# Mixture of experts in a four-layer kernel: routed groups of 384 rows through DRAM in place of every expert for every token

## The reference

```
scores = sigmoid(xt @ gate_w.T)                     # 4096 tokens, 16 experts
_, idx = top_k(scores + gate_b, 4)
w = take_along_axis(scores, idx);  w = 2.5 * w / sum(w)
comb[token, idx] = w                                # 0 for the 12 others
for e in 16 experts:
    h = silu(xt @ w1_e.T) * (xt @ w3_e.T)           # 128 hidden
    y = y + comb[:, e] * (h @ w2_e.T)
y = y + shared expert(xt)
```

## Time and profile before

| what | us |
|---|---|
| median of 3 runs | 1736.63 (1736.21 to 1738.77) |
| the profiled execution | 1737.69 |
| its span, first to last instruction | 1735.9 |
| TensorE busy | 1439.8 (83%) |
| VectorE busy | 1275.1 (73%) |
| ScalarE busy | 636.4 (37%) |
| GpSimd busy | 326.5 (19%) |
| mean granted TensorE clock, share of full speed | 0.93 |

### The profile page before, as it was taken

The page is one execution under the profiler, slowest core; times in us unless marked ns, Lnnn a source line. Parts: engine busy times, 40 slices in busy tenths (PEclk is TensorE's granted clock), DMA queues, the critical chain, the costliest instruction groups (busy, mean ns, idle before and its releaser), DMA issues. The chain is left out here.

```text
span 1735.9 us, 33621 instructions
## 1 busy us (share of the span) xinstructions
PE 1439.8 (83%) x10080; PEld 756.7 (44%) x10080; DVE 1275.1 (73%) x2834; ACT 636.4 (37%) x936; POOL 326.5 (19%) x340
## 2 busy tenths in 40 slices
PE   4799955999999999999997947887878788888766
PEld 2455532555555555555554522332333233232455
DVE  4999855878787777877667637887878788785475
ACT  0455531111111111111113412665656666666530
POOL 2433332112111121111002050111111111111110
PEclk7999976999999999999998965999999999899998
DMA  5011000000000000000004761111211111110002
GB/s 182 19 37 36 19 1 0 0 0 0 0 0 0 0 0 0 0 0 0 1 0 131 213 170 34 34 34 47 55 35 34 50 51 34 33 34 2 1 0 97
DMA packets 54738, 60.00 MB, mean 35 GB/s; under 512 B 6398, under 2 KB 41982, under 8 KB 54666
## 3 DMA queue, kind: packets, MB, share of 16 engines
q1 hardware_dynamic: 49466, 54.62, 11.1%
q10 hardware_dynamic: 5200, 4.33, 0.8%
HBM read 36.34 MB, written 22.28 MB: 34 GB/s over the span
## 5 line engine op out<-in xcount | busy, mean ns | idle before, releaser
L1461 DVE TENSOR_REDUCE small<-ps 128x1 f32<-128x480 f32 (+6 forms) x768 | 419.2, 596 | 99.7 <-PE ps L1513 91.4
L1439 ACT ACTIVATE region<-ps 128x1024 f32<-128x1024 f32 (+5 forms) x384 | 322.9, 880 | 229.9 <-PE ps L1570 228.2
L956 PE MATMUL ps<-region 128*128 (+1 forms) x1632 | 378.5, 382 | 8.0 <-issue 7.5
L788 ACT ACTIVATE region<-ps 128x512 f32<-128x512 f32 x136 | 81.2, 597 | 446.8 <-PE ps L960 408.8
L956 PEld LDWEIGHTS ps<-region 128*128 (+1 forms) x1632 | 158.9, 98 | 178.4 <-issue 15.9
L1586 PE MATMUL ps<-region 128*32 128x512 f32 (+5 forms) x1792 | 196.7, 512 | 28.3 <-POOL region L1411 21.6
L970 PE MATMUL ps<-region 128*128 (+1 forms) x1632 | 201.7, 273 | 19.6 <-DVE region L896 18.1
L1513 PE MATMUL ps<-region 48*128 48x480 f16 (+6 forms) x896 | 158.7, 344 | 45.6 <-DVE small L1461 44.8
L970 PEld LDWEIGHTS ps<-region 128*128 128x128 f16 x1632 | 156.7, 98 | 63.1 <-DVE region L896 19.4
L1411 POOL TENSOR_SCALAR_AFFINE_SELECT region<-region 128x512 f32<-128x512 f32 (+2 forms) x160 | 87.7, 549 | 491.5 <-ACT region L1439 491.5
L1570 PE MATMUL ps<-region 50*128 50x512 f16 (+5 forms) x896 | 133.7, 334 | 12.7 <-issue 10.5
(11 more groups left out here) (196 smaller groups left out, 1708.6 us busy)
## 6 DMA issues: line engine op xcount, KB each, us to landing
v_parts<-region SPq DMA_DIRECT2D x16, 576.0 KB, 5.8
region<-v_parts SPq DMA_DIRECT2D x16, 576.0 KB, 3.9
region<-k_parts SPq DMA_DIRECT2D x96, 68.0 KB, 2.2
region<-q_parts SPq DMA_DIRECT2D x96, 64.0 KB, 2.1
k_parts<-region SPq DMA_DIRECT2D x16, 272.0 KB, 3.3
x_sb<-in_x ACTq DMA_DIRECT2D x8, 512.0 KB, 9.4
region<-in_w13T SPq DMA_DIRECT2D x16, 256.0 KB, 2.9
q_parts<-region SPq DMA_DIRECT2D x16, 256.0 KB, 3.3
```

Source lines behind the costliest of these rows:

```text
L956: ins = nc.tensor.matmul(o, w(wt, kh, half_), xt[:, kh, cols], start=n == 0, stop=n == 5)
L1439: nc.scalar.activation(dst, src, ACT.Exp, scale=SCALE).then_inc(s_exp, 1)
L1461: nc.vector.tensor_reduce(nmp[:, qt, half, p0:p0 + np_, place], bank[:, 0:np_ * nk].rearrange("p (h k) -> p h k", h=np_), AX.X, ALU.max).t ...
```

## The change

The router now also keeps, for each token, its four experts and their weights. Each token's normalised row (high and low part, 256 words), its four experts and its number are one row of 261 words. The 16 experts have a region each in a DRAM tensor `xs`; a running count says at which place of its expert's region a token's row belongs, and GpSimd scatters the row to its four places with indirect DMAs, 128 rows each, 16 for a chunk. The shared expert alone is computed for all tokens, in the same loop over the 8 chunks. When all rows are in DRAM, tables are made from the counts: for each of 58 groups of 384 rows its expert and its first row (58 is the most that 16 x 1024 rows of 16 experts can need; a group beyond the last points at a spare region that holds no token). SyncE fills the end of each region with empty rows and loads the groups into 4 buffers. For a group TensorE does 12 transposes, 12 gate and up matmuls of 384 columns and 9 down matmuls with the weights of the expert, whose number it reads into a register. VectorE finds where each row's result belongs (`homes`), and GpSimd scatters the 384 results to `ys` with 3 indirect DMAs; rows of no token are dropped by the bounds check. The relayout then fetches the four results of each token (2 MB for a chunk) and adds them to x, each by its weight, before it normalises (`combine`).

The diff, cut; ScalarE's part, the router's arithmetic and the tables are left out:

```diff
+GROUP = 3 * P
+GROUPS = (B * L * TOPK + E * (GROUP - 1)) // GROUP
+ROW = D + TOPK + 1
+ROW_BUFS = 4
+G_BUFS = 4
+Y_BUFS = 3
...
             @block.sync
+                for b in range(ROW_BUFS):
+                    sp.wait_ge(s_sent[b], CHUNKS // ROW_BUFS * TC * TOPK * 16)
+                sp.wait_ge(s_tabs, 3)
+                def fill_tail(e):
+                    first = sp.value_load(tail_tab[0:1, e:e + 1], ...)
+                    sp.dma_start(xs[bass.ds(first, GROUP), :]..., flat(fill)).then_inc(s_tail[e], 16)
+                for e in range(FILLS_AHEAD):
+                    fill_tail(e)
+                for g in range(GROUPS):
+                    if g + FILLS_AHEAD < E:
+                        fill_tail(g + FILLS_AHEAD)
+                    if g < E:
+                        sp.wait_ge(s_tail[g], 16)
+                    if g >= G_BUFS:
+                        sp.wait_ge(s_gTps, g - G_BUFS + 1)
+                        sp.wait_ge(s_home, g - G_BUFS + 1)
+                    first = sp.value_load(start_tab[0:1, g:g + 1], ...)
+                    sp.dma_start(flat(xg[:, g % G_BUFS]), xs[bass.ds(first, GROUP), :]...)
...
             @block.gpsimd
+                for c in range(CHUNKS):
+                    if c + 2 < CHUNKS:
+                        rstd_of(c + 2)
+                    pool.wait_ge(s_slot, c + 1)
+                    for j in range(TC):
+                        for r in range(TOPK):
+                            nc.gpsimd.indirect_dma_start(out=xs, ..., in_=rows[:, b, j, :], ...).then_inc(s_sent[b], 16)
+                for g in range(GROUPS):
+                    b = g % Y_BUFS
+                    pool.wait_ge(s_home, g + 1)
+                    pool.wait_ge(s_yout, g + 1)
+                    for j in range(GT):
+                        nc.gpsimd.indirect_dma_start(
+                            out=ys, out_offset=bass.IndirectOffsetOnAxis(ap=home[:, b, j:j + 1], axis=0),
+                            in_=y_out[:, b, j, :], in_offset=None, bounds_check=B * L * TOPK - 1,
+                            oob_is_err=False).then_inc(s_back[b], 16)
...
             @block.vector
+                for c in range(CHUNKS):
+                    choose(c)
+                    if c + 2 < CHUNKS:
+                        statistics(c + 2)
+                    hidden(c)
+                    slots(c)
+                    hidden_low(c)
+                    if c + 2 < CHUNKS:
+                        normalised(c + 2)
+                    add_shared(c)
...
+                def homes(g):
+                    b, v = g % G_BUFS, g % 2
+                    dve.wait_ge(s_xg[b], (g // G_BUFS + 1) * 16)
+                    order.mark(nc.vector.scalar_tensor_tensor(out=which[:, v], ...))
+                    order.wait()
+                    order.mark(nc.vector.tensor_reduce(rank_of[:, v, :], which[:, v], AX.X, ALU.add))
+                    order.wait()
+                    if g >= Y_BUFS:
+                        dve.wait_ge(s_back[g % Y_BUFS], g // Y_BUFS * GT * 16)
+                    nc.vector.tensor_tensor(home[:, g % Y_BUFS, :], rank_of[:, v, :], ...).then_inc(s_home, 1)
+                def group_hidden(g):
+                    dve.wait_ge(s_gsilu, g + 1)
+                    nc.vector.scalar_tensor_tensor(out=hg_buf[:, g % 2, :], in0=ps[...], ...).then_inc(s_gh, 1)
+                    dve.wait_ge(s_ghh, g + 1)
+                    nc.vector.tensor_tensor(hgl[:, g % 2, :], hg_buf[:, g % 2, :], hgh[:, g % 2, :],
+                                            ALU.subtract).then_inc(s_ghl, 1)
+                def group_out(g):
+                    dve.wait_ge(s_gy, g + 1)
+                    nc.vector.tensor_copy(y_out[:, g % Y_BUFS]..., ps[:, 6:8, :]...).then_inc(s_yout, 1)
+                homes(0)
+                homes(1)
+                group_hidden(0)
+                for g in range(GROUPS):
+                    if g + 2 < GROUPS:
+                        homes(g + 2)
+                    if g + 1 < GROUPS:
+                        group_hidden(g + 1)
+                    group_out(g)
...
             @block.tensor
+                for g in range(GROUPS):
+                    now = ahead
+                    if g + 2 < GROUPS:
+                        group_transposes(g + 2)
+                    if g + 1 < GROUPS:
+                        ahead = expert(g + 1)
+                        group_gate_up(g + 1, ahead)
+                    group_down(g, now)
...
+                def fetch(c):
+                    pool.wait_ge(s_comb, c * TC * TOPK + 1)
+                    nc.gpsimd.dma_start(yg[:]..., ys[0:B * L * TOPK, :]...).then_inc(s_yg, 16)
...
+                def combine(c):
+                    dve.wait_ge(s_yg, (c + 1) * 16)
+                    for r in range(TOPK):
+                        for j in range(TC):
+                            if r:
+                                hold(dve, s_comb, c * TC * TOPK + 1 + n - TC + 1, s_tick)
+                            nc.vector.scalar_tensor_tensor(out=tile_of(c * TC + j), in0=yg[:, j, r, :], scalar=w,
+                                                           in1=tile_of(c * TC + j), op0=ALU.mult, op1=ALU.add).then_inc(s_comb, 1)
                 def normalise(order, b, h):
+                    combine(b * 2 + h)
```

More of the change, by code:

```diff
@@ L747, in flamingo, with flat @@
             CHUNKS = 2 * B
[L748 to L764, removed]
+            def flat(t):
+                return t.rearrange("p a n -> p (a n)")
@@ L766, in _, with rstd_of @@
             @block.gpsimd
             def _(pool):
[L768 to L772, removed]
+                def rstd_of(c):
+                    pool.wait_ge(s_var, c + 1)
+                    nc.gpsimd.tensor_tensor(rstd[:], ve[:], half[:], ALU.pow).then_inc(s_rstd, 1)
@@ L774, in _ @@
+                for b in range(Y_BUFS):
+                    pool.wait_ge(s_back[b], len(range(b, GROUPS, Y_BUFS)) * GT * 16)
             @block.scalar
             def _(act):
[L776 to L806, removed]
@@ L941, in comb_transposed @@
[L941 to L952 removed]
+                three = ((0, 0), (1, 0), (0, 1))
@@ new lines, in transposes @@
+                def transposes(c):
+                    if c:
+                        pe.wait_ge(s_xT, 2 * c)
+                    for part in range(2):
+                        pe.wait_ge((s_hi, s_lo)[part], c + 1)
+                        for k in range(KH):
+                            for j in range(TC):
+                                ins = nc.tensor.transpose(xT_ps[part][:, k, j * P:(j + 1) * P],
+                                                          halves(rows, c % ROW_BUFS)[:, j, part, k * P:(k + 1) * P], identh[:])
+                        ins.then_inc(s_xTps, 1)
@@ new lines, in _ @@
+                transposes(0)
+                logits(0)
+                for c in range(CHUNKS):
+                    shared_gate_up(c)
+                    ranks(c)
+                    if c + 1 < CHUNKS:
+                        transposes(c + 1)
+                        logits(c + 1)
+                    shared_down(c)
+                pe.wait_ge(s_slot, CHUNKS)
+                nc.tensor.matmul(count_ps, counts[:, CHUNKS, :], onesb[:, 0:1], start=True, stop=True)
+                nc.tensor.matmul(row_ps, onesb[:, 0:1], counts[:, CHUNKS, :], start=True, stop=True).then_inc(s_count, 1)
@@ new lines, in group_gate_up @@
+                def group_gate_up(g, e):
+                    pe.wait_ge(s_gT, 2 * g + 2)
+                    if g >= 2:
+                        pe.wait_ge(s_gh, g - 1)
+                    for half_ in range(2):
+                        n = 0
+                        for kh in range(KH):
+                            for part, low in three:
+                                w = flat((w13h, w13l)[low][:, bass.ds(e, 1), kh * D + half_ * P:kh * D + half_ * P + P])
+                                ins = nc.tensor.matmul(ps[:, 2 + 2 * (g % 2) + half_, 0:GROUP], w, xgT[:, g % 2, part, kh, :],
+                                                       start=n == 0, stop=n == 5)
+                                n += 1
+                    ins.then_inc(s_ggu, 1)
@@ new lines, in group_down @@
+                def group_down(g, e):
+                    pe.wait_ge(s_ghl, g + 1)
+                    if g:
+                        pe.wait_ge(s_yout, g)
+                    for j in range(GT):
+                        for n, (part, low) in enumerate(three):
+                            ins = nc.tensor.matmul(ps[:, 6 + j // 2, (j % 2) * D:(j % 2 + 1) * D],
+                                                   (hgh, hgl)[part][:, g % 2, j * P:(j + 1) * P],
+                                                   flat((w2h, w2l)[low][:, bass.ds(e, 1), :]), start=n == 0, stop=n == 2)
+                    ins.then_inc(s_gy, 1)
```

579 lines of the change are left out of this document (376 added, 203 removed).

## The result

The changed kernel takes 1881.8 us (median of 4 runs, 1879.7 to 1883.2) against 1736.4 before: 1.083 times as long, 95% interval 1.082 to 1.085. The forecast was 1911 us, with a range of 1745 to 2120 and a chance of 0.83 for slower.

The account below looks back on a forecast made before the run. TensorE was taken to bound the experts' stage before the change, GpSimd's scatters and a chain of waits after it. 243.1 + 191 + 12 + 540 + 824.6 + 100 = 1910.7 us of span, so 1911 us; range 1745 to 2120.

Parts of the forecast that it names:

- A: Router and shared expert, 8 chunks: GpSimd's 16 scatters per chunk set the pace, 20.5 us a chunk, 191 us in all.
- behind A: Between router part and groups: SyncE waits for every scatter, stores tails and loads the first group, 12 us.
- C: The 58 groups: scatters, landing, homes, hidden layer and eviction form a chain without overlap, 9.1 us a group, 540 us.
- D: Relayout: single-buffered fetches of 2.1 MB and four additions per token add 100 us, bounds 80 and 140.
- The unseen price: The time one scatter of 128 rows holds GpSimd: taken as 1.2 us, ends 0.42 and 2.0.
- The clock: In the groups: TensorE at its lower clock level needs 7.8 us a group, under the 9.1 us period, so doesn't decide.
- The DMA engines: In the groups about 0.8 MB move in 9.1 us; engines busy over 80% there or in A would show the forecast wrong.
- The rule on GpSimd's descriptors: VectorE's fast operations block GpSimd's DMA descriptors: in the router part at most 1.4 us a chunk, 11 us in all.
- Cheap scatters: Rival, same chain in the groups: a scatter takes 0.42 us, period 6.3, total 1719 us, faster; chance 0.14.
- 3t + L: In the groups: three scatters' GpSimd time plus the last one's landing; under 3.5 us, cheap scatters would decide.
- Dear ones: Rival: a scatter takes 2.0 us and its landing 3, period 12.1 us, sum 2187 + 2; chance 0.14.
- the third rival: In the groups: no chain holds, TensorE paces them at 5.1 us with a register load, total 1680 us; chance 0.03.

## Why the prediction was right

The sign, the mechanism and, within 1.6%, the time were right; that the time came so near is partly luck, since several terms were off in opposite directions. By the forecast's own steps, in us of span:

| part | forecast | measured |
|---|---|---|
| A, to SyncE's first tail (443.1) | 191 | 200 |
| behind A, to the first rows of a group (453.6) | 12 | 10.5 |
| C, to the relayout (960.1) | 540 | 506.5 |
| D, the relayout's addition | 100 | 98.8 |
| the rest, against before | 0 | -3.6 |

*The unseen price* was 1.2 us for a scatter. It is 0.96 + 0.30 = 1.26 in A and 1.28 in C: the chosen row (0.55 for GpSimd's smallest work) and the engines' 0.50 for 128 rows gave the size, but for a wrong reason, since 64 rows cost 0.92. In A it makes 8 x 16 x 0.06 = 8 of the 9 us that were missing; the first scatter started at 268.6, 25.5 us into the stage in place of 24, and makes the rest. Scatters that were held up (5.2 us in all, below) and roots that don't fall into this part (five are there, of eight forecast) cancel out.

*Part C*, step by step: scatters 3.55 (forecast 3.6); landing 1.55 in place of 2.4; from `homes` to the end of `group_out` 2.65 in place of 3.0; then 0.88 us from the eviction's end to the scatter's start (0.87 to 0.91 in 54 of the 58 groups), where I had a hop of 0.1. Sum 8.63 against 9.1. Two terms were mis-sized in opposite directions: the landing taken from SyncE's stores of 256 KB was 0.9 too long, and GpSimd's start 0.8 too short. Over all groups: 55 periods of 8.61 in place of 9.1 are 27 us less. No wait follows the last three, which take 11.3 us in place of 27.3: 16 less. Filling the pipeline took 14.4 (453.6 to 468.0) in place of 12, and 7.0 us at the block's end, 953.1 to 960.1, were not in the forecast. Together 33.5 less.

*The clock.* At the lower level TensorE was to need 7.8 us for a group, under the period, and so decide nothing. In the groups it was granted 0.83 and was busy for 58%; moving the wait, which added no speed to TensorE, took the period to 3.88 and the clock to 1.00. The step held. One sign did not: TensorE was to be busy for less than half, and was for 58%. A group took it 279.2 / 58 = 4.8 us at that clock, in place of 3.9; at a granted 1.00, with the moved wait, it was 3.7. It stayed off the path all the same.

*The DMA engines.* They were to stay under 80%. They had a share of 0.28 in A and 0.26 in the groups, but 0.83 (276 GB/s) in the 26 us between, with the first loads and tails. The forecast set 0.8 MB in 9.1 us, 87 GB/s, at less than half of the relayout's 171; it is just over half, and 82 were measured.

*Part D.* 33 us before the first q matmul and 67 behind it were forecast (61, and 6 for the clock). The first q matmuls after the change:

```profile
1007.97 2.31 PE L1463 MATMUL ps<-region 128*128 128x512 f16 x5 [3.41 <-DVE region L1412]
```

That is 47.9 us behind the block's start (960.1), where 47 were forecast, in place of 14.6: 33 more. From there to the attention's first load it is 155.4 us in place of 89.8 (925.9 to 1015.8), 66 more. Both parts held. Inside the second the shape was otherwise: the first stores of q in two successive batches lie 44.5, 43.5 and 30.0 us apart, where 46, 40 and 40 were forecast, and the first store stands 21.5 us behind the first matmul, before the change 9.7, since the fetch and the additions of the next chunk come ahead of the splits on VectorE.

*The rule on GpSimd's descriptors.* In four of the eight chunks of A a scatter is held up behind the subtraction that makes the low part (L959). Timeline of the kernel after: first a scatter beside the subtraction that is not held up, then, a chunk later, two that are, the first beside a normalisation (L954):

```profile
292.83 1.30 DVE L959 TENSOR_TENSOR region<-xn,region 128x1024 f16<-128x1024 f32 x1 [1.12 <-ACT region L875]
292.87 0.96 POOL L853 DMA_INDIRECT expert_rows<-region,small  x1 [0.30 <-issue]
...
311.36 1.41 DVE L954 TENSOR_SCALAR xn<-x_sb,mv,rstd 128x256 f32<-128x256 f32 x4 [7.17 <-POOL rstd L835]
311.52 1.16 POOL L853 DMA_INDIRECT expert_rows<-region,small  x1 [0.20 <-issue]
...
313.95 1.23 DVE L959 TENSOR_TENSOR region<-xn,region 128x1024 f16<-128x1024 f32 x1 [1.18 <-ACT region L875]
314.25 1.77 POOL L853 DMA_INDIRECT expert_rows<-region,small  x1 [0.30 <-issue]
```

A scatter that starts 0.3 us into the subtraction takes 1.77 us in place of 0.96, and one beside the normalisation 1.16: 1.0 us for each of these four chunks. Two scatters that start within 0.04 us of the subtraction's start take their 0.96, and the subtraction takes 1.30 and 1.26 in place of 1.23. Over all 128 scatters of A the time above 0.96 is 5.2 us, inside the 11 that the forecast named for this rule and did not put into its sum. It named the normalisations, which cost 0.20 of it each; the larger part is the subtraction. The Trainium skill, SBUF — State Buffer, "SBUF: two separate sides", has VectorE and GpSimd share a pair of ports as an exclusive lock, taken by whichever starts first, for VectorE operations in a two-port mode and also for those with two SBUF inputs, the latter only against a GpSimd operation that reads SBUF. The trace agrees with the latter: both inputs of L959 lie in SBUF, the scatter reads its indices there, the four late ones end 0.8 us after the subtraction does (316.02 against 315.18), and with the two that start together it is the subtraction that is longer. No run here varies it. The 0.62 us that the page gives for a DMA alone, in "A bandwidth-pool intuition that's wrong", is not what an indirect one takes here: 0.96.

*The rivals.* Cheap scatters (3t + L under 3.5 us) fell: 3.55 + 1.55 = 5.1. Dear ones fell too. What the third rival described, groups without the chain, is what the kernel with the moved wait does, but at 3.88 us and paced by GpSimd, not at 5.1 by TensorE.

## What to carry to other kernels

A ring of buffers overlaps only what its wait leaves free: for each wait ask which iteration it is for, and where on the waiting engine the instruction stands that lets that iteration start. A wait hoisted ahead of the work it doesn't protect undoes part of what buffers give: three gave a period of 8.6 us, four 4.8, and three with the wait at its place 3.9. Splitting the small index buffer from the large result buffer and waiting at the large one's writer gave back 256 of 1882 us at no memory to speak of. And where rows go through DRAM with indirect DMAs, count instructions (1.3 us each here, with 64 as with 128 rows of 1 KB) and the reading and summing at the other end: here 302 scatters and 99 us of relayout against 240 us of TensorE's time saved.

## What the runs showed that I had not expected

- An indirect DMA holds GpSimd for 0.92 us with 64 rows and 0.98 with 128, and the next one starts 0.30 us later.
- From the end of the VectorE operation that releases it, a scatter takes 0.87 to 0.91 us to start in 54 of 58 groups. Three scatters are seen as landed 1.2 to 2.1 us after the last one's end (median 1.5), with four result buffers 1.2 to 3.5 (median 2.5).
- A scatter starting 0.3 us into a VectorE subtraction of two SBUF operands took 1.77 us in place of 0.96; starting with it, 0.96.
- The attention stage, untouched, took 14 us longer in the run with 50 groups than after the change; that stays open.
